# Two expert stages opened without spent transposes, spent transposes placed elsewhere, and expert loads moved one stage on

## What is computed

```python
h = _L0_tok_ref(x, ...)                      # embedding windows, convolution
h = h + _L0_attn_ref(_layernorm(h), ...)     # linear attention
h = h + _L0_ffn_ref(_layernorm(h), ...)      # an expert chosen per segment, two layers
h = h + _L1_attn_ref(_layernorm(h), ...)     # attention with batch norm
h = h + _L1_ffn_ref(_layernorm(h), ...)      # 8 experts of width 128, top 2 of a router
h = h + _L2_attn_ref(_layernorm(h), ...)     # windowed attention with rotary turns
h = h + _L2_ffn_ref(_layernorm(h), ...)      # 8 experts of width 64, top 2 of a router
h = h + _L3_attn_ref(_layernorm(h), ...)     # long convolution through spectra
h = h + _L3_ffn_ref(_layernorm(h), ...)      # half of the tokens through an MLP
```

```python
logits = xn @ Wr + br                        # router, 8 experts
w = softmax(top_k(logits, 2))                # two weights a token
for e in range(8):
    y += (gelu(xn @ W1[e] + b1[e]) @ W2[e] + b2[e]) * w_full[..., e, None]
```

## Time and profile before

| | us |
|---|---|
| median of 3 runs | 812.21 |
| the three runs | 812.11, 816.56, 812.21 |
| the profiled execution, its own time | 819.01 |
| its span (what the trace covers) | 817.1 |
| outside the span | 1.9 |

### The profile page before, as it was taken

How to read it: one execution, slowest core, us unless ns; L and a number is a source line. 1 busy time by engine, 2 the same in 40 slices (tenths; PEclk the granted TensorE clock), 3 DMA queues, 4 the chain that set the end, 5 groups by cost and what they waited for, 6 DMA issues and landing times. The chain is left out here.

```text
span 817.1 us, 13076 instructions
## 1 busy us (share of the span) xinstructions
PE 638.4 (78%) x4688; PEld 424.8 (52%) x4688; DVE 533.5 (65%) x1442; ACT 330.4 (40%) x638; POOL 245.2 (30%) x217
## 2 busy tenths in 40 slices
PE   3497565774889778999988999988787787998864
PEld 3365444653767442232267887876232224984653
DVE  1034789654374578778945888484848886843897
ACT  1032211352555545545514465321243289831542
POOL 6612911414030011001025766441300177300420
PEclk9688879787999765989989999697689889999987
DMA  6854430102000010000010000004000000000011
GB/s 209 272 157 109 119 85 1 68 2 56 1 0 2 1 69 1 0 2 1 0 36 7 13 13 8 12 2 129 0 1 1 19 16 1 2 4 1 0 27 26
DMA packets 18944, 30.05 MB, mean 37 GB/s; under 512 B 6466, under 2 KB 15810, under 8 KB 18242
## 3 DMA queue, kind: packets, MB, share of 16 engines
q1 hardware_dynamic: 16322, 19.80, 8.7%
q0 software_dynamic: 2560, 9.44, 3.7%
HBM read 27.25 MB, written 1.05 MB: 35 GB/s over the span
## 5 line engine op out<-in xcount | busy, mean ns | idle before, releaser
L166 POOL TENSOR_TENSOR norm_rstd<-norm_var,minus_half 128x16 f32<-128x16 f32 x16 | 47.2, 2953 | 323.7 <-DVE norm_var L160 323.7
L1309 ACT ACTIVATE m_g<-PS,w_slot 128x512 f32<-128x512 f32 x96 | 60.8, 685 | 72.8 <-PE PS L1363 72.7
L1363 PE MATMUL PS<-m_xT,w_slot 64*128 64x512 f32 x192 | 71.5, 699 | 6.4 <-ACT m_g L1309 6.3
L1251 DVE TENSOR_TENSOR m_gw<-m_g,PS 128x512 f32<-128x512 f32 x96 | 61.0, 676 | 18.7 <-PE PS L1371 9.2
L1387 PE MATMUL PS<-m_gw,w_slot 128*64 128x512 f32 x192 | 58.1, 675 | 1.2 <-DVE m_gw L1251 1.2
L106 PE MATMUL PS<-w_base 128*128 128x128 f32 x316 | 45.8, 299 | 7.9 <-PEq L2737 7.2
L106 PEld LDWEIGHTS PS<-w_base 128*128 128x128 f32 x316 | 40.0, 156 | 12.4 <-issue 10.7
L267 PE MATMUL PS<-w_base,tok_windows 128*128 128x128 f32 x128 | 22.0, 334 | 24.3 <-issue 12.2
L328 DVE COPY tok_windowsT<-PS 128x512 f32<-128x512 f32 x16 | 11.1, 691 | 41.9 <-remote 22.0
L1371 PE MATMUL PS<-m_gT,m_sel 48*128 48x512 bf16 x96 | 24.3, 421 | 17.1 <-DVE m_gw L1251 11.4
L2151 ACT COPY rat_xf<-PS 64x512 f32<-64x512 f32 x32 | 33.3, 1042 | 9.0 <-PE PS L2204 8.6
(11 more groups left out here) (341 smaller groups left out, 1635.6 us busy)
## 6 DMA issues: line engine op xcount, KB each, us to landing
rff_routed<-in_routed SPq DMA_DIRECT2D x64, 129.0 KB, 2.0
w_slot<-in_w_rat SPq DMA_DIRECT2D x1, 1525.0 KB, 11.2
w_slot<-in_w_win SPq DMA_DIRECT2D x1, 1378.5 KB, 5.8
w_slot<-in_w_m SPq DMA_DIRECT2D x1, 1329.0 KB, 5.7
w_slot<-in_w_early SPq DMA_DIRECT2D x1, 1092.0 KB
rat_inv<-in_rat_taps SPq DMA_DIRECT2D x1, 1024.0 KB, 7.4
rat_hf<-in_rat_taps SPq DMA_DIRECT2D x1, 1024.0 KB, 7.5
out<-H SPq DMA_DIRECT2D x8, 128.0 KB, 2.2
```

What stands on the lines that cost most here:

```text
L166: nc.gpsimd.tensor_tensor(N.rstd[:], N.var[:], C.minus_half[:], ALU.pow).then_inc(S["norm_rstd"], 1)
L1251: nc.vector.tensor_tensor(gw[:, i % 2, half, :], g[:, i % 2, half, :], gate_bank[half], ALU.mult)\
L1309: nc.scalar.activation(g[:, i % 2, half, :], hid_bank[(n - 1) % 3], ACT.Gelu, bias=b1[:, s:s + 1])\
L1363: nc.tensor.matmul(hid_bank[n % 3], w1[lane(half), s, :], pair_of(xT, pair)[lane(half)], start=True, stop=True).then_inc(S["hid_ps"], 1)
```

## The change

Five edits, none of which changes what is computed.

1. In `gelu_moe` the spent transposes at the start are gone. `turn_x(0, 1)` writes a second bank, `opening_bank`, and so needs no wait for the copy of the first half; `copy_x(0, 1)` reads it there. The waits for `sel` and `b2_split` move from ahead of `turn_x` to ahead of `gates(0)`, and that for `identb` to ahead of `turn_parts(0)`.
2. In the same opening, spent transposes are issued between `hidden(0)` and `hidden(1)` (10 in m1, 24 in m2) and between `turn_parts(0)` and `gates(0)` (8 in each).
3. Spent transposes are issued at the end of four stages: 16 in `batchnorm_attention`, 10 in m1 and 10 in m2 (one line), 8 in `window_attention`.
4. SP issues the loads of expert chunks 2 and 3 in `linear_attention` and no longer in `token_convolution`.
5. In `rational_convolution` PE issues `forward(s)` ahead of `numerators(s)`.

```diff
--- before.py
+++ after.py
@@ -230,7 +230,7 @@
             C.load(sp, "early")
             C.load(sp, "gate")
             sp.wait_ge(gathered[5], 16 * G4)
-            C.experts.load(sp, (0, 1, 2, 3))
+            C.experts.load(sp, (0, 1))
 
         @block.gpsimd
         def _(pool):
@@ -368,7 +368,7 @@
 
         @block.sync
         def _(sp):
-            C.experts.load(sp, (4, 5, 6, 7))
+            C.experts.load(sp, (2, 3, 4, 5, 6, 7))
 
         @block.gpsimd
         def _(pool):
@@ -1026,6 +1026,7 @@
                 ins.then_inc(S["y_ps"], 1)
             for s in range(4, SQUARED_TAIL):
                 denominators(s)
+            rouse(nc, C, PS[0][:, 0, :], 16)
 
 
 
@@ -1137,6 +1138,7 @@
         banks = [PS[k // 2][:, k % 2, :] for k in range(2 * W)]
         hid_bank, gate_bank, y_bank, ahead_bank = banks[0:3], banks[3:5], banks[5:7], banks[7]
         spare_banks = [gate_bank, y_bank]
+        opening_bank = hid_bank[2]
         ahead_logits = ahead_bank[:, 0:W * G4 * E8]
         lane = lambda half, n=D: slice(half * D, half * D + n)
         steps = [(pair, s) for pair in range(NP) for s in range(SL)]
@@ -1276,12 +1278,12 @@
 
             def copy_x(it, k):
                 act.wait_ge(S["xT_ps"], it * 2 + k + 1)
-                out = pair_of(xT, it * 2 + k)
+                out, x_bank = pair_of(xT, it * 2 + k), opening_bank if (it, k) == (0, 1) else ahead_bank
                 if again:
-                    ins = nc.scalar.activation(out, ahead_bank, ACT.Identity, bias=C[pre + "_beta"],
+                    ins = nc.scalar.activation(out, x_bank, ACT.Identity, bias=C[pre + "_beta"],
                                                scale=C[pre + "_gamma"])
                 else:
-                    ins = nc.scalar.copy(out, ahead_bank)
+                    ins = nc.scalar.copy(out, x_bank)
                 ins.then_inc(S["xT"], 1)
 
             def exponentials(it):
@@ -1323,16 +1325,15 @@
             ident = C["ident"]
             w1 = C[pre + "_w1"].rearrange("p (s n) -> p s n", s=SL)
             w2 = C[pre + "_w2"].rearrange("p (s f) -> p s f", s=SL)
-            rouse(nc, C, y_bank[1], 24 if again else 44)
 
             def turn_x(it, k):
                 for w in (2 * k, 2 * k + 1):
                     pe.wait_ge(S["normed"], it * W + w + 1)
-                    if k:
+                    if it and k:
                         pe.wait_ge(S["xT"], it * 2 + 1)
                     for u in range(U):
                         at = (w % 2 * U + u) * P
-                        ins = nc.tensor.transpose(ahead_bank[:, at:at + P],
+                        ins = nc.tensor.transpose((opening_bank if (it, k) == (0, 1) else ahead_bank)[:, at:at + P],
                                                   xn[:, w, 2 * u:2 * u + 2, :].rearrange("p g f -> p (g f)"), ident)
                 ins.then_inc(S["xT_ps"], 1)
 
@@ -1396,9 +1397,6 @@
 
             pe.wait_ge(C.sem("base"), C.count("base"))
             pe.wait_ge(C.sem(pre), C.count(pre))
-            pe.wait_ge(S["sel"], 1)
-            pe.wait_ge(S["identb"], 1)
-            pe.wait_ge(S["b2_split"], 5)
             for k in range(2):
                 turn_x(0, k)
             logits(0)
@@ -1406,11 +1404,16 @@
                 for s in range(SQUARED_TAIL, STEPS):
                     C.denominators.transform(pe, C, s, spare_banks[s % 2])
             hidden(0)
+            rouse(nc, C, opening_bank, 10 if again else 24)
             hidden(1)
+            pe.wait_ge(S["identb"], 1)
             turn_parts(0)
             if again:
                 pe.wait_ge(C.denominators.moved, STEPS)
+            rouse(nc, C, gate_bank[1], 8)
             pe.wait_ge(S["gT"], W)
+            pe.wait_ge(S["sel"], 1)
+            pe.wait_ge(S["b2_split"], 5)
             gates(0)
             for i, (pair, s) in enumerate(steps):
                 if i == n_round - 1:
@@ -1431,6 +1434,7 @@
                     if plan.parts == i:
                         turn_parts(1)
             turn_output(NP - 1)
+            rouse(nc, C, hid_bank[0], 10)
             pe.wait_ge(S["h_new"], NP)
 
 
@@ -1883,6 +1887,7 @@
             ladder([(58, turn_x), (71, keys_values), (80, queries), (146, turn_k), (161, turn_q), (173, scores),
                     (198, turn_prob), (213, lambda c: weigh_values(c, 0)), (223, lambda c: weigh_values(c, 1)),
                     (243, turn_output), (260, output)], 57, then)
+            rouse(nc, C, PS[0][:, 1, :], 8)
 
 
 def gelu_moe_64(nc, H, PS, C, dram):
@@ -2207,8 +2212,8 @@
                 ins.then_inc(S["xf_ps"], 1)
 
             for s in range(STEPS):
+                forward(s)
                 numerators(s)
-                forward(s)
             pe.wait_ge(S["ht"], 2 * STEPS)
 
             for g in range(PAIRS // 2):
```

## The result

The changed kernel took 799.28 us (median; 797.29 to 803.85) beside 812.56 us of the kernel before: a ratio of 0.9831, 95% interval 0.9807 to 0.9855. Repeated twice later it gave 0.9827 (0.9788 to 0.9867) and 0.9851 (0.9821 to 0.9881). The kernels of one comparison ran on one chip beside their own runs of before; on one kind of chip before took 812.6 to 813.9 us in the median, on another 818.3 and 819.4, so ratios are compared, and microseconds only within a comparison.

A forecast was written before the change was run, and what follows sets the result against it. No engine was full over the whole program (PE busy 78%); the change touches stage openings and ends, where engines wait in a chain. Terms summed to −4.5 us, 819.01 to 814.5, median 812.21 to 807.7; forecast 807.5, range 801 to 814.

The forecast's parts named there:

- the one on the expert loads: Token stage's end: SP issues eight loads less, but DVE ends at 77.60 after SP's 77.12, so no gain.
- The linear stage's term: Linear stage: later loads let POOL's addition of chunk 4 hold DVE for its length; +1.5 us (−0.6 to +3.6).
- m1: m1's opening: logits 2.8 us sooner, later PE work slower, `turn_parts` −2.0 us (−1.4 to −3.4); stage end +0.4.
- m2: m2's opening: without the 44 spent transposes ahead, `turn_parts` comes sooner, −5.9 us (−4.3 to −6.3); stage end +0.3.
- the transposes at stage ends: Ends of four stages: they cost what they outlast DVE's last work by; batch norm +0.3, window +0.4, m1 +0.4, m2 +0.3.
- The rational stage: `rational_convolution`: `forward` first starts ACT about 2 us sooner but delays numerators; +0.5 us (−1 to +2.9).
- Rival E: Loops of m1 and m2: new openings leave PE at clock 0.50 deeper in, ending slower, about 821 us; chance 0.05.
- Rival B: Openings and loads: removed transposes save 2.8 us more, loads gain 0.6; 802.8 us, or 801.3 with rational's good end; chance 0.26.
- rival C: Linear and rational stages: POOL holds DVE (+2.1), numerators' delay passed on whole (+2.4); 812.2 us, no change; chance 0.21.
- Rival D: m2's opening: transposes do not raise the clock, so its 24 run at 0.50 (+1.6); 809.3 us; chance 0.03.

The follow-up runs named there:

- e4: The kernel before, unchanged, profiled a second time; one time of 812.65 us.
- e7: The changed kernel with the additions of the shared matrix cut in four quarters; ratio 0.9888 to before.
- e17: The changed kernel with three chunks loaded in the token stage, additions of the shared matrix in quarters and `numerators` ahead of `forward`; 808.15 us, 0.9866.
- e3: The changed kernel without the spent transposes at the four stage ends, first time; ratio 0.9834 to before.
- e12: The changed kernel without the spent transposes at the four stage ends, repeated beside the changed kernel on one chip; 799.74 us, 0.9811.
- e10: The changed kernel without spent transposes inside the openings or at the four stage ends, beside the changed kernel on one chip; 810.36 us, 0.9952.
- e8: The changed kernel without spent transposes inside the openings or at the four stage ends, first time; ratio 0.9994 to before.
- e5: The changed kernel without the spent transposes inside the two openings, first time; ratio 0.9905 to before.

## Why the prediction was wrong

**The step that failed is the one on the expert loads**: "its last issue ends at 76.78 + 0.34 = 77.12 while DVE ends at 76.85 + 0.75 = 77.60: no gain there." The rows are right and the margin is 0.48 us, in an execution in which DVE had idled 9.1 us and ACT 9.2 us at one stretch earlier in that stage, and PE 12.2 us in four. In e4, at 812.65 close to the median, those engines end at 63.6, SP at 71.95 and the stage at 73.1, and with 16 or 24 loads it ends at 66 to 68: 6 to 7 us where the forecast put nothing. The kernel doesn't keep all of it, since the linear stage is 6 us longer in some executions. Edit 4 alone is worth 2.1 us (e2), and undone in the changed kernel it costs about 3 (e1's ratio of 0.9868 against 0.9831 and 0.9827), where the forecast had a loss of 1.5. That is 3.6 to 4.8 of the 8.6 us by which the forecast missed; the two expert stages, below, hold another 4.2 to 4.4.

Two signs stood in the numbers. The profiled execution took 819.01, 6.8 more than the median, and I subtracted that from the end of the sum instead of asking which stage held it. And SP, with a load each 1.1 to 1.2 us from about 37 us on, was the only queue busy without a break to the end of a stage that it could end; the question "who is last if this one is 10 us earlier" was never put. After a margin of half a microsecond the term's range should have reached the whole delay.

**The linear stage's term** (+1.5, −0.6 to +3.6) had its mechanism right: chunk 3 was expected at 20.1 us into the stage and chunk 4 at 29.2, and their additions began at 19.2 to 20.0 and 28.8 to 29.5. POOL did hold DVE for an instruction's length. It was mis-sized since I looked for one collision; there can be two, at chunk 3 as well, and the stage is 70.6 to 72.4 without and 77.5 to 78.4 with both: nothing or nearly 6 us, and seldom between.

**m1** (−2.0, with −1.6 after its end's transposes): −4.1. The router products cost 3.60 us at 0.50, a little over what was expected (3.2 to 3.4), but the turning before was done at the high clock, and `turn_parts` came after 15.3 us, 1.3 sooner than the forecast's 16.6; about 1 us more is the loop's, which the forecast gave nothing: the low stretches of the stage sum to 17 us for 27 before. How much of this is chance in the clock's timing e7 and e17 tell, where the same opening and loop took 110.6 and 112.8 us.

**m2** (−5.9, with −5.6): −7.5. Logits after 4.9 us (5.5 to 6 said), `turn_parts` after 11.8 (12.5 to 14.7). Both stages came out shorter for the same missed step: the transposes at stage ends were counted as cost only (+0.3, +0.4, +0.4 and m2's), where the 16 in `batchnorm_attention` and the eight in `window_attention` hand their clock on to `turn_x`. Without them (e3 and e12) `turn_parts` came after 15.8 us in m1 and 13.2 in m2; but the stages are only 0.5 and 0.1 us longer than in the changed kernel's first profile, so most of those microseconds are lost again behind. Their cost was put too low where it can be told: batch norm 100.2 without the 16 and 100.8 with them, against +0.3 and at most +0.5.

**The rational stage** (+0.5): 102.2 (e4) to between 102.9 and 103.4, inside what the clock does to it; the sign agrees with the like-with-like numbers above.

**Rival E**, that the new openings leave PE low in the loops, is refuted by the windows: m1's clock rose to 0.93. The part of it that is true stands in e10: an opening without any spent transposes is nearly as short, and the kernel gains next to nothing by it in the end (0.9952, where edit 4 alone has 0.9966). **Rival B** was nearest, 801.3 to 802.8, for partly wrong reasons: it gave the loads 0.6 us. The first half of **rival C**, POOL holding DVE, is what the dear linear stages show, at more than the price it was given; its second half, numerators passed on at 2.4 us, is not seen in any rational stage.

**Rival D**, that transposes don't raise the clock, is refuted once more: in after, `turn_x` follows 16 spent transposes and takes 0.13 us for each of eight; in e3 and e8, where the 16 are missing, 0.24 (1.94 for eight).

## What to carry to other kernels

A stage ends with its last queue, and an engine that only issues DMAs is one: write down for each stage when every queue ends, and by how much the last leads; a lead of half a microsecond in one execution tells nothing. When the profiled execution is 1% above the median, find the stage that holds the difference before adding anything up. And two edits that each cost little to undo (1.4 and 5.2 us) can cost 12 us undone together: judge such fillers by a table of two by two on one chip.

## What was not expected of the hardware

There are two token stages, by the chip and not by the kernel (two chips of each kind among the runs with a known chip): 66 to 68 us (16 or 24 loads; 73 with 32) in thirteen profiles, and 79 in seven, the first profile of before among them. Window of e8 and, for comparison, of e4, at the same time of the stage:

```profile
31.00:39.00 8.00, 0.00 (x0) 0.00 (x0) 0.00 (x1) 0.01 (x1) 5.36 (x6) 0.58 0.82 238
```

```profile
31.00:39.00 8.00, 8.00 (x66) 5.99 (x65) 2.43 (x4) 2.55 (x6) 6.17 (x7) 1.00 0.81 237
```

The DMA traffic is the same (238 and 237 GB/s), and PE has no instruction in the one and 66 in the other. The gathers are issued alike in both, one each 1.25 us, up to 37 us; some records of PE and of landings are missing in these profiles, so what PE waits for is not known. On such a chip edit 4 can't gain at the stage's end, where DVE ends at 77.2 to 77.6: the kernels lie about 3 us nearer to before there (e5 and e8 0.9905 and 0.9994, the same kernels 0.9867 and 0.9952 on the other). That the times of the first comparison came from one kind of chip and its profile from the other fits 819.01 beside 812.21, but wasn't shown.

The stage lengths, too, come in a few sharp values instead of a spread (m1 114.6 in seven profiles of four kernels, window 137.6, 140.8 or 144.4), and what differs between two values of the window stage is the length of one stretch at clock 0.50.
